# Newton's rounds of two group norms on GpSimd: fourteen one-step operations rewritten as seven two-step operations

## What is computed

```
def _gn(v, G=32, eps=1e-05):          # group norm: 4 channels and all pixels of an image
    g = v.reshape(B_, H_, W_, G, C_ // G)
    m = jnp.mean(g, axis=(1, 2, 4), keepdims=True)
    s = jnp.var(g, axis=(1, 2, 4), keepdims=True)
    return ((g - m) / jnp.sqrt(s + eps)).reshape(v.shape)

x = x + attention(_gn(x))             # shifted 7x7 windows, 8 heads of 16, rel. position bias, mask, softmax, proj
x = x + conv3x3(_gn(x))               # weights: magnitude aware signs, 128 -> 128 channels, padding SAME
return x
```

## Time and profile before

| what | value |
|---|---|
| time, median of 3 runs | 3491.44 us (3483.04 to 3496.02) |
| the profiled execution | 3491.2 us, its span 3489.4 us |
| mean granted TensorE clock | 0.981 |
| PE busy | 3214.1 us (92%) |
| DVE busy | 2902.3 us (83%) |
| ACT busy | 2450.3 us (70%) |
| POOL busy | 2295.0 us (66%), 3683 instructions |

### The profile page before, as it was taken

The page is one execution under the profiler, slowest core; times in us unless marked ns, Lnnn a source line. Parts: engine busy times, 40 slices in busy tenths (PEclk is TensorE's granted clock), DMA queues, the critical chain, the costliest instruction groups (busy, mean ns, idle before and its releaser), DMA issues.

```text
span 3489.4 us, 154043 instructions
## 1 busy us (share of the span) xinstructions
PE 3214.1 (92%) x64139; PEld 2700.3 (77%) x64139; DVE 2902.3 (83%) x6143; ACT 2450.3 (70%) x5473; POOL 2295.0 (66%) x3683
## 2 busy tenths in 40 slices
PE   2899999999999999999999999999999999999996
PEld 1678778778878778878778878778878778788785
DVE  5688888888888888888888888888888888888885
ACT  1777777777767777777777767777767777777772
POOL 4476666776666776666766666766667766657764
PEclk9999999999999999999999999999999999999998
DMA  2112211222211222211222211222111222112111
GB/s 59 37 45 53 49 43 48 51 51 53 50 41 48 51 51 53 51 40 48 52 49 53 49 41 48 49 52 52 45 45 47 51 52 50 43 45 51 33 36 36
DMA packets 352643, 165.99 MB, mean 48 GB/s; under 512 B 148048, under 2 KB 351952, under 8 KB 351952
## 3 DMA queue, kind: packets, MB, share of 16 engines
q1 hardware_dynamic: 351952, 156.13, 18.4%
HBM read 53.31 MB, written 51.38 MB: 30 GB/s over the span
## 4 chain that ended last, share of the span: by engine, by line
PE 58%; DVE 17%; POOL 12%; issue 9%; ACT 2%; SPq 1%; DMA 0%; DVEq 0%; POOLq 0%; ACTq 0%
PE conv_ps L997 15%; PE qkv_ps L879 11%; PE scores_ps L892 8%; PE probsT_ps L903 7%; PE attn_ps L916 5%; PE attn_ps L920 4%; PE misc_ps L968 4%; DVE s_sb L750 4%; DVE plane_lo L762 3%; POOL s_sb L435 3%; PE misc_ps L959 2%; DVE s_max L755 2%; PE misc_ps L965 2%; POOL plane L462 2%; POOL gn_t L419 1%
## 5 line engine op out<-in xcount | busy, mean ns | idle before, releaser
L435 POOL TENSOR_TENSOR s_sb<-s_sb,s_max 113x392 f32<-113x392 f32 x1024 | 959.6, 937 | 1019.5 <-DVE s_max L755 1018.8
L497 ACT COPY probsT<-probsT_ps 128x392 f32<-128x392 f32 x1024 | 495.1, 483 | 365.6 <-PE probsT_ps L903 348.7
L490 ACT ACTIVATE probs<-s_sb 113x392 f32<-113x392 f32 x1024 | 553.2, 540 | 174.6 <-POOL s_sb L435 172.1
L462 POOL TENSOR_TENSOR plane<-x_n 128x224 f32<-128x224 f32 x896 | 640.7, 735 | 18.7
L903 PE MATMUL probsT_ps<-ident,probs 113*128 113x113 f32 x4096 | 587.8, 266 | 70.0 <-ACT probsT L497 70.0
L755 DVE TENSOR_REDUCE s_max<-s_sb 113x8 f32<-113x392 f32 x1024 | 574.5, 561 | 35.2
L750 DVE TENSOR_TENSOR s_sb<-scores_ps,bias 113x392 f32<-113x392 f32 x1024 | 565.7, 552 | 36.7 <-PE scores_ps L892 29.8
L558 ACT COPY v<-qkv_ps 64x256 f32<-64x256 f32 (+2 forms) x1280 | 390.2, 324 | 217.9 <-PE qkv_ps L879 211.9
L903 PEld LDWEIGHTS probsT_ps<-ident,probs 113*128 113x128 f32 x4096 | 434.6, 142 | 125.8 <-ACT probs L490 84.3
L997 PE MATMUL conv_ps<-plane_hi,wc_hi 128*128 128x224 f16 x2688 | 487.1, 264 | 24.4 <-DVE conv_y L824 20.3
L997 PE MATMUL conv_ps<-plane_hi,wc_lo 128*128 128x224 f16 x2688 | 480.6, 262 | 0.0
(11 more groups left out here) (138 smaller groups left out, 6364.6 us busy)
## 6 DMA issues: line engine op xcount, KB each, us to landing
x_in<-in_x_dram SPq DMA_DIRECT2D x224, 224.0 KB, 3.1
recip_wide<-recip SPq DMA_DIRECT2D x1024, 49.0 KB
out_dram<-x_out SPq DMA_DIRECT2D x224, 224.0 KB, 2.3
x<-in_L_conv_w_dram SPq DMA_DIRECT2D x1, 576.0 KB
x<-L_conv_pruning_mask_dram SPq DMA_DIRECT2D x1, 576.0 KB
x_n<-_conv_rel_pos_table_dram SPq DMA_DIRECT2D x14, 10.7 KB
x_n<-in_mask_dram SPq DMA_DIRECT2D x1, 196.0 KB
plane<-n_L_conv_qkv_weight_dram SPq DMA_DIRECT2D x1, 192.0 KB
```

The source lines that it names most:

```text
L435: nc.gpsimd.tensor_tensor(s, s, top, ALU.subtract).then_inc(sub_ready, 1)
L462: last = nc.gpsimd.tensor_tensor(plane[:, t % 2, j], *sums[j])
L490: nc.scalar.activation(probs[0:QP, slot % 2, :, :, 0:N], s_sb[0:QP, slot % 4], ACT.Exp)\
L497: nc.scalar.copy(probsT[:, g % PT_SLOTS], probsT_ps[:].rearrange("p (w n) -> p w n", n=ODD)[:, :, 0:N])\
```

## The change

Newton's round is written as two `tensor_scalar` operations with two arithmetic steps each, t = (y * y) * half and y = (t + 1.5) * y, in place of four `tensor_tensor` operations; the shift is one operation in place of two. The second operand and the third are tiles of one column, read as scalars for each partition. A block of a norm has seven operations where it had fourteen, and six waits where it had thirteen. The order on every engine is the same, and so are the values up to rounding.

```
             def newton(gn, img):
 
-                tt = nc.gpsimd.tensor_tensor
+                ts = nc.gpsimd.tensor_scalar
                 done = [0]
 
                 def then(ins):
                     done[0] += 1
                     ins.then_inc(gn.newton, 1)
-                    pool.wait_ge(gn.newton, img * (4 * NEWTON + 1) + done[0])
+                    pool.wait_ge(gn.newton, img * 2 * NEWTON + done[0])
 
                 pool.wait_ge(gn.ready_steps, (img + 1) * 3)
                 for _ in range(NEWTON):
-                    then(tt(gn.t[:], gn.y[:], gn.y[:], ALU.mult))
-                    then(tt(gn.t[:], gn.t[:], gn.half[:], ALU.mult))
-                    then(tt(gn.t[:], gn.t[:], three_halves[:], ALU.add))
-                    then(tt(gn.y[:], gn.t[:], gn.y[:], ALU.mult))
-                then(tt(gn.shift[:], gn.kept_out[:], gn.mean[:], ALU.subtract))
-                tt(gn.shift[:], gn.shift[:], gn.y[:], ALU.mult).then_inc(gn.ready, 1)
+                    then(ts(gn.t[:], gn.y[:], gn.y[:], gn.half[:], ALU.mult, ALU.mult))
+                    then(ts(gn.y[:], gn.t[:], three_halves[:], gn.y[:], ALU.add, ALU.mult))
+                ts(gn.shift[:], gn.kept_out[:], gn.mean[:], gn.y[:], ALU.subtract, ALU.mult).then_inc(gn.ready, 1)
```

## The result

The changed kernel takes 3407.0 us (median of 4 runs, 3404.6 to 3410.3), the kernel before 3489.7 on the same chip (3483.0 to 3496.0): ratio 0.976, 95% interval 0.974 to 0.979. The forecast was 3389, the range 3366 to 3440. The profiled execution after has a span of 3408.5 us, 80.9 less than before, and a mean granted TensorE clock of 0.995 in place of 0.981.

A forecast was written before the change was run, and what follows sets the result against it. The prediction took GpSimd's Newton blocks as serial time of the whole kernel. gn2's blocks 26.6, gn1's 27.5 and the clock's falls 48 sum to 102 us off 3491.4, giving 3389 us, range 3366 to 3440.

The forecast's parts named there:

- The block is serial time: All fourteen GpSimd operations of each of the 64 Newton blocks are serial time of the whole kernel.
- The new operation, 0.34 us: One-column tensor_scalar on GpSimd with two scalars from memory: 0.34 us, range 0.30 to 0.36, against 0.19 for the old.
- The wait after it, 0.08: Wait on GpSimd's own semaphore behind each new operation: 0.08 us, as behind the old ones.
- the gn2 block: Second norm's Newton block: 2.86 us against 3.69, 0.83 less, all passed on; 32 times, 26.6 us.
- gn1's block: First norm's Newton block, two operations held up by VectorE: 0.86 us saved (0.6 to 1.3), 27.5 us in all.
- a sign of being wrong: The prediction is wrong if PE's gaps do not shrink by what the blocks do.
- The clock, 48 us: TensorE's clock falls behind gn1 stops no longer come once PE's gap shrinks from 2.15 to 1.29 us: 48 us.
- the 6.8 us kind of fall: Deeper clock fall behind eight gn1 stops: priced at 2.9 us each, by 1.9 times the low time.
- The first: Clock falls behind gn1 as before, only the blocks' 54 us come: 3437 us, chance 0.09.
- The second: Another chain, VectorE or GpSimd falling behind later, loses half of the blocks' 54 us: 3416 us, chance 0.06.
- Rival 3: One-column tensor_scalar in the blocks takes 0.19 us like the old form: 3334 us, chance 0.04.
- rival 4: Slower: the new operation takes over 0.46 us, blocks get longer; at 0.6 us, 3597 us, chance 0.04.

The follow-up runs named there:

- pad_gn1: The changed kernel with two added one-column tensor_tensor operations at the head of every gn1 block: 3412 us.
- pad4_gn1: The changed kernel with four added one-column tensor_tensor operations at the head of every gn1 block: 3502 us.
- gn1_only: The kernel before with the new seven operations in gn1's blocks only, the old fourteen kept in gn2's: 3480 us.
- pad1_gn2: The changed kernel with one added one-column tensor_tensor operation at the head of every gn2 block: 3421 us.

## Why the prediction was right, and where not

- **The block is serial time.** Right: longer and shorter blocks moved PE's gaps by what they changed, except where DVE's operations took or gave something (`pad_gn1`). Images without a fall say it free of the clock: 0.50 us shorter with gn1's blocks changed, 0.63 with gn2's, 1.09 with both.
- **The new operation, 0.34 us.** Right, 0.343, out of the row of nine columns. The shift was 0.373.
- **The wait after it, 0.08.** Mis-sized: 0.10. Six times 0.02 and 0.03 for the shift make the gn2 block 3.03 us instead of 2.86, and its gain 0.66 instead of 0.83: 21 us over the kernel, not 26.6.
- **gn1's block.** Its shape was right (two operations met, not three; 3.69 us forecast 3.6). What `x_n` pays in meeting `plane_lo` was mis-sized: 0.47, more than the 0.38 taken as the most. Net 0.52 instead of 0.86: 17 us, not 27.5. So PE's gap there shrank by 0.49, to 1.66 and not to 1.3, while the block shrank by 0.99, which the prediction had named as a sign of being wrong. The Trainium skill ("SBUF — State Buffer", section "Who interferes with whom") has the first to issue keep the port; by it `x_n`, whose record starts 0.07 us before `plane_lo`'s, would have paid nothing. The trace shows the reverse, `x_n` longer and `plane_lo` at its usual 0.62. In `pad4_gn1` even a one-column operation whose record starts 0.14 us before `plane_lo`'s takes 0.81 us instead of 0.34, and `plane_lo` 0.62. Which was issued first at the port no record shows, so the page may hold; as a forecast from starts in a timeline it did not.
- **The clock, 48 us.** The number was right, the reason for it wrong, so it came right by luck. The step "gaps of 1.52 behind gn2 were never followed by a fall, so a gap of 1.29 is not either" took 31 stretches of one execution for a property of the gap. `gn1_only` had 18 falls behind the same gaps. What the runs show instead: behind gn1, falls came at gaps of 2.15 us (17 and 23 of 30, by kernel) and 2.79 (29 of 30), never at 1.66 or 1.74; behind gn2, at 2.1 (26 of 31), at about 1.55 (0, 4 and 18 of 31, by kernel), 1.43 (13 of 31), twice in `pad1_gn2` at 1.33 and 1.59, never where most gaps are 0.92. So the length below which no fall came is not the same at the two places, and the change pulled both gaps under it at once. Had gn2's gain been 0.3 us smaller, some falls would have stayed, as in `pad1_gn2`; the margin was narrower than forecast. Why the same gap has no fall in one kernel and 18 in another, and why 1.66 behind gn1 never has one, stays open. Of the price, the 6.8 us kind of fall was put at 2.9 us by its low time; the image of before that holds the first one lasts 1081.91 - 975.37 = 106.54 us, 3.18 more than one without a fall, and the sum would be 50.
- **Rivals.** The first (the clock falls as before) did not happen, but either half of the change alone keeps 17 or 18 falls. The second (a chain close behind) did not show: images are 102.27 us apart, 1.09 less than before, where the two blocks' net sum is 1.16. Rival 3 (0.19 us, like the old form) is refuted by 0.343 us, and so is rival 4 (over 0.46).

Sum as measured: 21 + 17 + 48 = 86 by terms, 81 in the span.

## What to carry to other kernels

Half the operations are not half the time: here a two-step operation with its wait cost 0.443 us against 0.27 for a one-step one, and paid only because it replaced two of them (0.54). When a chain through PE is full of short stops, count what the clock does behind them, and count it in more than one kernel: a stop that the clock never fell behind in one kernel can have falls in the next, at the same length. Ask of a serial block first whether it can run in idle time and whom it stands in front of; one cast moved by a unit gave half as much as this whole change.

## What was not expected of the hardware

- The second scalar read from memory adds 0.075 us to a one-column GpSimd `tensor_scalar` (0.268 with one, 0.343 with two); `tensor_tensor` takes 0.19.
- The wait on GpSimd's own semaphore is 0.10 us after these, 0.08 after `tensor_tensor`.
- Two added operations of 0.27 us each lengthened PE's gap behind gn1 by 0.08 us, four by 1.13: how many of POOL's operations meet VectorE's with two SBUF inputs changed with their place, and with it the price.
- With one gap of 2.1 us in place of 0.92 and 0.57, PE had 26 falls of the clock to 1.2 GHz where it had none; with the longer images that cost 67 us, though the same work was done.
- In `gn1_only` the clock fell 1.6 to 2.1 us after PE's gap had ended and PE was busy again, and behind gaps as short as 1.31 us; 180 gaps of 1.64 to 1.75 us behind gn1, in six kernels, had no fall.
